# A four-block kernel on one core: block ends without a drain on POOL, and one loop over all units on POOL

## Time and profile before

| | us |
|---|---|
| median of three timed runs | 1512.23 |
| profiled execution | 1508.08 |
| its span, first to last instruction | 1506.3 |
| `layer0` | 0 to 993.6 |
| `route_and_convolve` | 993.6 to 1179.2 |
| `experts` | 1179.2 to 1467.7 |
| `combine` | 1467.7 to 1506.2 |

### The profile page before, as it was taken

How to read it: one execution, slowest core, us unless ns; L and a number is a source line. 1 busy time by engine, 2 the same in 40 slices (tenths; PEclk the granted TensorE clock), 3 DMA queues, 4 the chain that set the end, 5 groups by cost and what they waited for, 6 DMA issues and landing times. The chain is left out here.

```text
span 1506.3 us, 29415 instructions
## 1 busy us (share of the span) xinstructions
PE 1309.6 (87%) x8092; PEld 669.3 (44%) x8092; DVE 997.9 (66%) x2343; ACT 868.9 (58%) x1661; POOL 554.0 (37%) x543
## 2 busy tenths in 40 slices
PE   5899999999999999999989998657884599999970
PEld 2433433434343343343433334234432488888770
DVE  1878888888888888888867885234443254444448
ACT  0277787788778778778867875212221244444332
POOL 2122342342343234224224215355555244444440
PEclk9999999999999999999989998779996799999995
DMA  6333222312312322231231232368773223222229
GB/s 222 105 97 111 91 73 73 107 55 70 107 55 74 110 92 72 71 108 55 70 108 52 75 94 68 94 219 282 254 245 99 77 71 90 78 65 66 62 58 334
DMA packets 116391, 162.27 MB, mean 108 GB/s; under 512 B 17874, under 2 KB 52370, under 8 KB 116051
## 3 DMA queue, kind: packets, MB, share of 16 engines
q1 hardware_dynamic: 103842, 137.73, 28.2%
q0 software_dynamic: 8448, 17.58, 3.4%
q10 hardware_dynamic: 4016, 6.05, 1.3%
HBM read 104.20 MB, written 49.77 MB: 102 GB/s over the span
## 5 line engine op out<-in xcount | busy, mean ns | idle before, releaser
L775 DVE TENSOR_REDUCE row_max<-ps_max 128x2 f32<-128x1024 f32 x512 | 614.9, 1219 | 137.2 <-PE ps_max L1032 133.5
L983 ACT ACTIVATE probs<-ps_exp 128x512 f32<-128x512 f32 x1024 | 556.3, 597 | 132.1 <-PE ps_exp L1032 114.1
L1032 PE MATMUL ps_exp<-q_op,k_op 32*128 32x512 f32 x1024 | 352.3, 502 | 26.9 <-ACT probs L983 19.9
L1032 PEld LDWEIGHTS ps_exp<-q_op,k_op 32*128 32x128 f32 x1024 | 145.9, 184 | 410.1 <-ACT probs L983 368.8
L1113 PE MATMUL ps_y<-probs,v_aug 128*32 128x512 f32 x2048 | 279.0, 617 | 0.2 <-ACT y_raw L989 0.2
L1032 PE MATMUL ps_max<-k_op,q_op 32*128 32x512 f32 x1024 | 255.4, 498 | 2.6 <-DMA k_op<-k_parts_scratch 1.6
L1579 ACT ACTIVATE hidden<-ps_h,b 128x256 f32<-128x256 f32 x268 | 118.7, 474 | 157.4 <-PE ps_h L1553 147.0
L1622 POOL DMA_INDIRECT y_scratch<-result,goes_to x134 | 128.4, 958 | 154.7 <-DVE result L1607 128.6
L671 POOL TENSOR_TENSOR rstd<-var_eps,minus_half 128x4 f32<-128x4 f32 x32 | 32.8, 1026 | 366.5 <-DVE var_eps L770 366.5
L315 POOL DMA_INDIRECT sorted_scratch<-rows,place x120 | 116.1, 967 | 88.8 <-issue 31.7
L1560 PE MATMUL ps_o<-w,hidden 128*128 128x128 f32 x1072 | 131.3, 276 | 0.0
(11 more groups left out here) (185 smaller groups left out, 1483.8 us busy)
## 6 DMA issues: line engine op xcount, KB each, us to landing
q_op<-q_parts_scratch SPq DMA_DIRECT2D x16, 1024.0 KB, 5.7
k_op<-k_parts_scratch SPq DMA_DIRECT2D x16, 1024.0 KB, 8.4
q_op<-k_pad_scratch SPq DMA_DIRECT2D x15, 1024.0 KB
k_op<-k_pad_scratch SPq DMA_DIRECT2D x15, 1024.0 KB
unit_rows<-sorted_scratch SPq DMA_DIRECT2D x136, 66.0 KB
q_parts_scratch<-qk_split SPq DMA_DIRECT2D x16, 512.0 KB, 3.1
k_parts_scratch<-qk_split SPq DMA_DIRECT2D x16, 512.0 KB, 2.9
q_parts_scratch<-qk_split SPq DMA_DIRECT2D x16, 256.0 KB, 2.4
```

The lines of the kernel that those rows point to most:

```text
L775: dve.tensor_reduce(row_max[group // 2][:, t, head:head + 2], ps_max[u][:, :, :], AX.X, ALU.max)\
L983: act.activation(probs[s % 2][:, i, :], ps_exp[i % 2][:, :], ACT.Exp).then_inc(exp_done, 1)
L1032: return pe.matmul(out, lhsT, rhs, start=True, stop=True)
```

## The change

All four blocks are opened with `no_gpsimd_drain=True`. In `route_and_convolve` POOL no longer loads nine numbers after its waits for its indirect DMAs; it waits for `units_ready` and loads `units[8]` alone, ahead of these waits. In `experts` POOL has one loop from 0 to that number in place of eight loops; the body is the same. The other engines keep their nine numbers and eight loops.

```diff
@@ -527,7 +527,7 @@ (layer0; the same edit in route_and_convolve L1323, experts L1511, combine L1650)
-        block = ctx.enter_context(nc.Block())
+        block = ctx.enter_context(nc.Block(no_gpsimd_drain=True))
@@ -1476,9 +1476,10 @@ (route_and_convolve, POOL)
             for b in batches:
                 route.scatter(pool, dram, b)
+            pool.wait_ge(units_ready, 1)
+            ends[pool] = pool.value_load(units[0:1, E:E + 1], min_val=E, max_val=MAX_UNITS)
             for p in range(ROW_SETS):
                 pool.wait_ge(route.scattered[p], 16 * SCATTERS * len(range(p, B, ROW_SETS)))
-            load_ends(pool)
@@ -1615,14 +1616,14 @@ (experts, POOL)
-            def one(e, n):
+            total = ends[pool]
+            with pool.Fori(0, total) as n:
                 for i in range(2):
                     pool.wait_ge(result_ready[i], n + 1)
                     apart(pool, pool_passed)
                     pool.indirect_dma_start(dram["y"], bass.IndirectOffsetOnAxis(goes_to[i][:, 0:1], 0), result[i][:, :], None)\
                         .then_inc(stored[i], 16)
 
-            total = over_units(pool, one)
             for i in range(2):
                 pool.wait_ge(stored[i], 16 * total + 16)
```

## The result

The changed kernel takes 1503.86 us (median of 10 runs) against 1512.55 us for the kernel before (10 runs), a ratio of 0.9941 with a 95% interval of 0.9925 to 0.9958: 8.7 us less by the medians, where the forecast was 14.7. A ratio is worked out from all runs and so can differ a little from the quotient of the medians; from here on its 95% interval stands behind it in brackets. Two later measurements, which stand among the experiments, gave 0.9925 and 0.9932. The mean of the three, 0.9933, is 10.1 us of 1512.55. Faster was right and the time lies inside the range, near its upper end; the size was too large by about 4.6 us.

The account below looks back on a forecast made before the run. The prediction saw a 13.5 us hole with no engine busy, filled by POOL's routing drain and register loads. Terms −1.6 − 11.1 − 2.0 = −14.7 us took 1512.2 to 1497.5 us; range 1492.5 to 1504.5.

Parts of the forecast that it names:

- End of `layer0`, 1.6 us: Block end of `layer0`: without POOL's drain, DVE opens the barrier 1.6 us sooner; bounds 0 and 1.6.
- End of `route_and_convolve`, 11.1 us: Routing block end: POOL's drain and eight loads go, SyncE is last; 11.1 us gained, the middle of 8.9 and 13.4.
- The 13.4 end: Routing block end: if only profiling slows SyncE, DVE and POOL open the barrier at 1165.7 in timed runs, gaining 13.4 us.
- the trace's own 8.9: Routing block end: SyncE arrives at 1170.1 as in the profiled execution, so 8.9 us go.
- End of `experts`, 2.0 us: Block end of `experts`: POOL's drain after its wait for the last results goes, 2.0 us, all on the path.
- One loop, 0 us: POOL's expert loop: set-ups hidden, stall should go (1.6 us), longer cadence may cost 2.6; bounds −4.2 and +1.0, taken 0.
- The drained work comes back: Rival, behind the routing barrier: POOL's next DMAs start late, up to 4.1 us return; 1497.5 to 1501.6 us; chance 0.12.
- The wait in another form: Rival, block ends: barrier or plain drain waits for the same thing; 1507.0 us, or 1512.2 if its end is fixed; chance 0.08.
- The long cadence: Rival, expert stage: units running at 3.79 us fall to 4.12, 16 of them, +5.3 us: 1502.8 us; chance 0.06.
- The back edge: Rival, POOL's one loop: each turn fetches code, 1.6 us per unit, +107 us with all 67: 1605 us; chance 0.02.

Follow-up runs that it names:

- routing flag alone: Changed kernel with POOL's drain left out only at the end of `route_and_convolve`, the other three drains kept; 1505.08 us, 0.9943 against the kernel before.
- late reads: Changed kernel with SyncE and ScalarE reading two numbers before the routing barrier, each further one ahead of its expert's loop; 0.9897, then 0.9869 against the kernel before.

## Why the prediction was right, and where it was not

**End of `layer0`, 1.6 us: right at the place.** From the end of POOL's last operation to the opening it is 2.43 us with the drain (before, drains put back, routing flag alone) and 0.87 without; 1.56 go, and DVE opens the barrier, as the earlier trace rows said. What the step missed is the next drain: I bounded this edit at 0 to 1.6 us, and by itself it is worth 8.4 (4.6 to 12.0 by its interval). In the whole change that makes no difference, since the routing drain goes as well; as the price of the part it is wrong by some five times.

**End of `route_and_convolve`, 11.1 us: the mis-sized term.** Who is late next was right (SyncE in all three traces of the changed kernel). The choice of the middle between 8.9 and 13.4 was not. From the end of POOL's waits to the barrier it is 13.6 us before and 7.9, 3.7 and 4.6 after, 5.4 in the mean: 8.2 go. The 13.4 end wanted SyncE undisturbed in timed runs, and the kernel that reads two numbers is faster in timed runs, so SyncE's nine still cost there. That is 2.9 of the 4.6 us that the forecast was too high; the trace's own 8.9 would have been the better choice. What slows SyncE stays open.

**End of `experts`, 2.0 us: right.** From POOL's last branch to the barrier it is 2.3 us with the drain and 0.2 without.

**One loop, 0 us: right sum, wrong reason.** The flags alone give the same time. But I read the 4 us idle of the earlier trace rows as POOL waiting for its own code at the start of the last expert and said that a shorter list should end it. The late half is the last write ahead of that start: POOL sets up its eighth loop (the last MOVE below) only at 1421.7, when the late write has left its sequencer. And not all of the excess is POOL's: it got past its wait for DVE, where L332 raises `pool_passed`, at 1418.3, so the write came 3.5 us behind that, where the one before it came after 0.8 (1416.0 to 1416.77). That is 2.7 us too many, not 3.2. From the kernel before, the set-ups of the eight loops, and L332 from 1416 to 1420 us:

```profile
L1518 POOLq MOVE  x8: 29/29/42, 1180.2 to 1421.7; - x8
```

```profile
L332 POOLq EVENT_SEMAPHORE  x2: 17/17/17, 1416.0 to 1418.3; - x2
```

The late write stands at the same half of the same unit with eight loops and with one, with ten more DMAs and with eight more scatters. That refutes my reading; the cause was not found. The Trainium skill (Runtime: NRT & Kernel Launch, Instruction fetch mechanics) lets a branch inside the two held blocks pay nothing. The three traces of the changed kernel agree: every write there that starts after 1.1 us and more of idle without a releaser is a second half, with no branch of the loop just ahead of it. So the rule does not explain the late one either.

**The sum.** With the measured parts it is 1.6 + 8.2 + 2.0 = 11.8 us, against 10.1 as the mean of three ratios, whose intervals reach from 6.4 to 14.5. The 1.7 us between them can't be resolved here.

**The rivals.** *The drained work comes back* fell at the place that I priced: POOL's first DMA starts 0.6 us after the barrier with and without the drain, no row numbers of the first unit wait for it, and the 8.31 us come a second time when the drain starts elsewhere. But something small does come back. The pause of 1.98 us at the 114th scatter is one part; POOL's next wait for ScalarE is 1.15 us there instead of 3.65, so it is caught up. In all six traces without the first two drains POOL also stands for 1.1 to 2.1 us, released by no engine, before the 88th, 96th and 104th write of the experts, and in none that has the routing drain. Where the usual idle is 0.82 us (late reads, second trace) it is 1.12 to 1.15: as an estimate from these rows 0.3 us each, 1 us in all, which may be part of what the sum misses; that is not shown. *The wait in another form* fell: no such row is left. *The long cadence* did happen in the profiled execution, but nothing shows that the change brought it. Its expert stage without drain is 291.8 us against 286.5 before, 5.3 us more, just that rival's price. But both forms show short and long ones: with eight loops it is 288.0 us (flags alone), 290.5 (the flag of `layer0`, drain taken off) and 291.6 (eight more scatters, drain taken off), with one loop from 282.7 (late reads, second trace) to those 291.8. *The back edge* fell: no cost per unit appears.

## What to carry to other kernels

A long drain of POOL at a block end is a cost that can be taken out where, as here, POOL has waited for its DMAs by semaphores, but what it returns is the distance to the next-latest engine, so read that engine's arrival and take the trace's own number until a run says otherwise. Don't price two drains apart: leave one out and look at how long the other becomes. Where the next engine is late by a row of register loads, move those behind the barrier; here that took another 5 us out of the trace and 7.6 out of the timed runs.

## What the runs showed of the hardware that I had not expected

- POOL's drain at a block end took 3.2 us behind 27 scatters (2.3 after POOL's last operation), 8.31 behind the 101 that followed that drain, 8.96 behind 109, 3.33 behind 125, 3.98 behind 133, and 2.04 behind 128 with no drain ahead of them. At the experts' end it was 2.02 us in every kernel that has it (134 indirect and 2 or 12 plain DMAs, and 101 scatters more where the routing end alone has no drain). POOL's waits for the DMAs had ended each time. The 0.08 us per scatter fits all drains behind fewer than 114 DMAs; the long ones end there, and the 114th DMA itself starts late in nine traces, though not in the two with 125 and 133. What POOL does at that count is open.
- In every kernel POOL writes the second half of unit 55 after 4.0 to 4.5 us of idle that ends with no engine's release.
- From the opening of `layer0`'s barrier to the end of POOL's waits at the routing end it took from 170.4 us (1166.3 - 995.9, flags alone) to 177.3 (1170.8 - 993.5, late reads). The expert stage spreads by 9 us, as told above. With such spreads one profiled execution can show 2.0 us of a gain of 10.
